# Attention written out over its 16 groups instead of a loop of three groups a pass

## The reference

```python
c_q = x @ W_dq
Q = (c_q @ W_uq).reshape(Bx, Sx, N_HEADS, D_K)
c_kv = x @ W_dkv
K = (c_kv @ W_uk).reshape(Bx, Sx, N_HEADS, D_K)
V = (c_kv @ W_uv).reshape(Bx, Sx, N_HEADS, D_K)
scores = jnp.einsum('bqhd,bkhd->bhqk', Q, K) / math.sqrt(D_K)
causal = jnp.tril(jnp.ones((Sx, Sx), dtype=bool))
scores = jnp.where(causal, scores, -jnp.inf)
attn = jax.nn.softmax(scores, axis=-1)
out = jnp.einsum('bhqk,bkhd->bqhd', attn, V).reshape(Bx, Sx, N_HEADS * D_K)
return out @ W_o
```

## Time and profile before

| | us |
|---|---|
| median of 3 runs | 1392.69 |
| lowest and highest run | 1389.38, 1393.0 |
| the profiled execution, its time | 1396.73 |
| the profiled execution, its span | 1395.0 |
| TensorE's first attention matmul of group 1, from the span's start | 527.38 |
| of group 3, the first in the loop | 588.83 |
| of group 12, the first behind the loop | 885.40 |
| of group 14, which has a list of its own | 947.64 |

### The profile page before, as it was taken

The page is one execution under the profiler, slowest core; times in us unless marked ns, Lnnn a source line. Parts: engine busy times, 40 slices in busy tenths (PEclk is TensorE's granted clock), DMA queues, the critical chain, the costliest instruction groups (busy, mean ns, idle before and its releaser), DMA issues. The chain is left out here.

```text
span 1395.0 us, 25999 instructions
## 1 busy us (share of the span) xinstructions
PE 1117.4 (80%) x7114; PEld 677.1 (49%) x7116; DVE 859.1 (62%) x2534; ACT 672.0 (48%) x1676; POOL 451.0 (32%) x456
## 2 busy tenths in 40 slices
PE   3548889884887599999899899999778289989860
PEld 2246777773333134444344344434256267778750
DVE  4773333333895688888788788888056743333327
ACT  3523434433456056766566566767636234444430
POOL 3635666663234400000000000000047456666640
PEclk9999999997778589999999999999989569999985
DMA  7602222224545903444434444340066012222229
GB/s 230 210 1 68 87 88 87 86 87 145 191 163 133 152 2 56 69 67 69 65 48 64 62 55 56 55 55 10 18 202 206 23 49 88 88 88 84 89 90 334
DMA packets 109455, 133.23 MB, mean 96 GB/s; under 512 B 30032, under 2 KB 83728, under 8 KB 109328
## 3 DMA queue, kind: packets, MB, share of 16 engines
q1 hardware_dynamic: 91280, 89.65, 28.6%
q0 software_dynamic: 13824, 37.77, 8.5%
q10 hardware_dynamic: 4224, 4.19, 0.9%
HBM read 82.68 MB, written 48.50 MB: 94 GB/s over the span
## 5 line engine op out<-in xcount | busy, mean ns | idle before, releaser
L1368 ACT ACTIVATE t_prob<-t_psS 128x512 f32<-128x512 f32 (+3 forms) x768 | 327.9, 494 | 191.0 <-PE t_psS L1300 160.1
L1388 DVE CUSTOM_DVE_ANT_0 t_psR<-t_psR,all_causal 128x128 f32<-128x128 f32 (+3 forms) x512 | 247.4, 503 | 63.6 <-PE t_psR L1278 58.9
L1278 PE MATMUL t_psR<-stacks_kst,stacks_qst 96*128 96x512 bf16 (+3 forms) x768 | 235.9, 347 | 32.7 <-PEq L851 16.1
L1297 PE MATMUL t_psS<-stacks_qst,stacks_kst 99*128 99x512 bf16 (+3 forms) x768 | 225.6, 334 | 2.2 <-ACT t_prob L1368 1.5
L1392 DVE TENSOR_REDUCE t_maxp<-t_psR 128x1 f32<-128x512 f32 x256 | 175.8, 687 | 20.9 <-PE t_psR L1278 20.6
L1278 PEld LDWEIGHTS t_psR<-stacks_kst,stacks_qst 96*128 96x128 bf16 x768 | 70.3, 98 | 214.3 <-DVE t_maxp L1388 108.0
L1311 PE MATMUL t_psO<-t_prob,t_vst 128*32 128x512 f32 (+3 forms) x1536 | 163.7, 498 | 3.0 <-ACT t_prob L1368 1.1
L1268 POOL COPY t_vst<-stacks_values 128x512 f32 (+1 forms) x16 | 9.8, 615 | 442.7 <-DMA stacks_kst<-qk_parts 442.4
L644 PE MATMUL ae_psG<-a_w,ae_xT 128*128 x432 | 116.4, 406 | 15.5 <-issue 9.8
L644 PE MATMUL be_psG<-b_w,be_xT 128*128 x432 | 117.4, 409 | 13.6 <-issue 9.1
L1300 PE MATMUL t_psS<-all_causal_t,all_ident_bf 128*128 128x128 bf16 x512 | 110.2, 222 | 0.0
(11 more groups left out here) (284 smaller groups left out, 1909.6 us busy)
## 6 DMA issues: line engine op xcount, KB each, us to landing
qk_parts<-q_parts SPq DMA_DIRECT2D x32, 384.0 KB, 2.6
stacks_qst<-qk_parts SPq DMA_DIRECT2D x96, 128.0 KB, 4.7
stacks_kst<-qk_parts SPq DMA_DIRECT2D x96, 128.0 KB, 7.1
q_yk<-y_rows SPq DMA_DIRECT2D x16, 512.0 KB, 6.0
s_yk<-y_rows SPq DMA_DIRECT2D x16, 512.0 KB, 9.3
o_rows<-t_orow SPq DMA_DIRECT2D x32, 136.0 KB, 7.6
bl_raw<-o_rows SPq DMA_DIRECT2D x8, 544.0 KB, 3.8
xn_rows<-al_xn SPq DMA_DIRECT2D x8, 512.0 KB, 3.9
```

The lines of the kernel that those rows point to most:

```text
L1278: nc.tensor.matmul(psR[bank][:, 0:w], qst[slot][0:KROWS, h, i * P:(i + 1) * P], kst[slot][0:KROWS, h, k0:k0 + w], start=True, stop=True).t ...
L1297: ins = nc.tensor.matmul(ps, kst[k][0:MROWS, h, j * P:(j + 1) * P], qst[k][0:MROWS, h, a:(c + 1) * 512], start=True, stop=a > j * P)
L1368: nc.scalar.activation(prob[j % 2][:, h, a:(c + 1) * 512], psS[n % ST_BANKS][:, a - c * 512:512], ACT.Exp, scale=DK ** -0.5).then_inc(exp_ ...
L1388: ins = nc.vector.tensor_tensor_reduce(psR[bank][:, 0:w], psR[bank][:, 0:w], T.causal[:, 512 - w:512], 1.0, -BIG, ALU.add, ALU.max, maxp[: ...
```

## The change

The loop is gone: every engine's code now goes over all 16 groups with the group number as a constant, so all waits compare with constants, no register is computed, and `hold` counts nothing. The planner's lists are made once and looked up. Tiles, banks, slots and the order of work stay as they were.

```diff
@@ phase_attention @@
+        plans = {(later, with_before): plan_step(units, later, with_before)
+                 for later, with_before in {(min(2, NG - 1 - g), g > 0) for g in range(NG)}}
...
             def run(eng):
-                last = (NG - 1) // SLOTS - 1
-                for k in range(SLOTS):
-                    step(k, k, 2, k > 0)
-                with eng.Fori(1, last) as it:
-                    for k in range(SLOTS):
-                        step(it * SLOTS + k, k, 2, True)
-                for g in range(last * SLOTS, NG):
-                    step(g, g % SLOTS, min(2, NG - 1 - g), True)
+                for g in range(NG):
+                    step(g, g % SLOTS, min(2, NG - 1 - g), g > 0)
             return run
...
         def ring_bank(g, idx):
-            return (idx + (ring_base(g) if isinstance(g, int) else RING0 - 2)) % RING_BANKS
+            return (idx + ring_base(g)) % RING_BANKS
...
-                for what, *at in plan_step(units, later, with_before)[0]:
+                for what, *at in plans[later, with_before][0]:
```

More of the change, by code:

```diff
@@ L1190, in run @@
             def run(eng):
-                last = (NG - 1) // SLOTS - 1
-                for k in range(SLOTS):
-                    step(k, k, 2, k > 0)
-                with eng.Fori(1, last) as it:
-                    for k in range(SLOTS):
-                        step(it * SLOTS + k, k, 2, True)
-                for g in range(last * SLOTS, NG):
-                    step(g, g % SLOTS, min(2, NG - 1 - g), True)
+                for g in range(NG):
+                    step(g, g % SLOTS, min(2, NG - 1 - g), g > 0)
             return run
         def ring_base(g):
-            if isinstance(g, int) and g == 0:
+            if g == 0:
                 return RING0
-            return g * RING + (RING0 - 2 - (AHEAD if isinstance(g, int) and g == NG - 1 else 0))
+            return g * RING + (RING0 - 2 - (AHEAD if g == NG - 1 else 0))
         def ring_bank(g, idx):
-            return (idx + (ring_base(g) if isinstance(g, int) else RING0 - 2)) % RING_BANKS
+            return (idx + ring_base(g)) % RING_BANKS
         def out_at(g, c):
-            if isinstance(g, int) and g == NG - 1:
+            if g == NG - 1:
                 return ring_base(g) + 2 + c + 1
-            later = min(2, NG - 2 - g) if isinstance(g, int) else 2
-            return ring_base(g + 1) + (plan_step(units, later, True)[1].index(("o", c)) + 1)
+            return ring_base(g + 1) + (plans[min(2, NG - 2 - g), True][1].index(("o", c)) + 1)
         @block.sync
@@ L1237, in step @@
                     load_max(g + 1, (k + 1) % SLOTS)
-                if not isinstance(g, int) or g + SLOTS < NG:
+                if g + SLOTS < NG:
                     hold(sp, pv_done, g * PV + PV, T)
@@ L1419, in step @@
                 base = ring_base(g)
-                for idx, (what, at, *ahead) in enumerate(plan_step(units, later, with_before)[1]):
+                for idx, (what, at, *ahead) in enumerate(plans[later, with_before][1]):
                     r, bank = base + idx, ring_bank(g, idx)
```

## The result

The changed kernel takes 1368.43 us (median of 4 runs, 1363.75 to 1371.37) against 1391.04 us of the kernel before in the same comparison (4 runs, 1384.49 to 1393.0). The ratio is 0.9839, with a 95% interval of 0.9811 to 0.9866: a gain of 22.6 us, by the interval 19 to 26. I had forecast 18.4 us, a time of 1374.3 and a range of 1369.5 to 1380.5.

A forecast was written before the change was run, and what follows sets the result against it. TensorE's matmuls bound written-out attention groups; the loop added steps and branch pauses. Of 20.0 us (7.7 register steps and holds, 11.9 way round, 0.4 late maxima), less 1.6 late maxima, 18.4 off 1392.69 gave 1374.3 us, range 1369.5 to 1380.5.

The forecast's parts named there:

- a shift of the phases behind attention by 3.6 us: Phases behind attention: one branch in their moved code gains or loses a pause, giving 1370.7 or 1377.9 us; chance 0.05.
- late maxima: Group starts in attention: 2 of 9 groups wait 0.78 us for DMAs of row maxima, 1.6 us off the gain.
- The price of the middle groups, by the written-out ones: Groups 3 to 11: each becomes a written-out group of 30.73 us, 20.0 us less than the 296.57 in the loop.
- Register arithmetic and counted holds: Loop groups 3 to 11: removing these steps on TensorE and VectorE saves 0.85 us a group, 7.7 us over nine.
- The bound of 2.6 us: VectorE in a loop group: removed register and semaphore instructions sum to 2.6 us, the most their removal could save.
- The way round: Groups 5, 6, 8, 9 around TensorE's two taken branches: 11.9 us go, 7.2 pauses and 4.7 lower clock.
- its cover: VectorE's loop branch, beside its wait for TensorE: counted at nothing; with that cover gone, 74 ns would be the price.
- Instruction loading: Attention written out as longer code: fetching it costed at nothing; should the cover be gone, 3.6 us and the clock behind.
- Late maxima in every group: Rival, SyncE's DMAs in attention: all nine groups start late, 7.0 us instead of 1.6, giving 1379.7 us; chance 0.15.
- hidden steps: Rival, loop groups: register steps were hidden all along, the 0.85 us a group stays, giving 1382.0 us; chance 0.05.
- a pause that is not the branch's: Rival, TensorE in attention: the pause recurs each third group whatever the branch and stays, giving 1386.2 us; chance 0.03.
- late blocks of code: Rival, TensorE's straight code: waits for blocks cost 6.0 us each, five give 1404.2 us, slower; chance 0.02.

## Why the prediction was right or wrong

**Where it failed: the other phases, put at nothing in the sum and at 3.6 us in the range.** The sum let every phase but attention stand still, and the range allowed the rest only this: the runs before lie 3.6 us apart, "which I allow on both sides of the forecast". The one rival of this kind, a shift of the phases behind attention by 3.6 us, looked the wrong way: behind attention 0.9 us came on, and ahead of it 7.7 us went, in code that the change doesn't touch. The time came out 5.9 us under the forecast of 1374.3. Of this 1.65 us is the base, whose median fell from 1392.69 to 1391.04 with a fourth run, and 4.2 us is a larger gain, 22.6 and not 18.4. About 1 of the 4.2 is the late maxima, below; the other 3 to 4 lie outside groups 3 to 11. Three runs had shown too little: with the fourth the kernel before spans 8.5 us (1384.49 to 1393.0), and the changed kernel 7.6.

On the other chips, where the phases ahead and behind lie within some 2 us of each other, the gain was 19.0 and 20.2 us by the medians (ratios 0.9856 and 0.9843). That the 3 to 4 us over the forecast are chance is argued, not shown, since the difference of 7.7 us was not reproduced and its cause stays open. What speaks for chance is the spread of this same code. The expert phase, from its first product into `psG` (line 644) to its last, takes 208.7 us ahead of attention and 207.5 behind it in the profile before, 205.2 and 206.5 in the one after. From the queries' first product to attention's it is 110.8 against 107.1 us there, and between 104.5 and 108.1 in the nine profiles on the other chips, where the kernels written out (106.4 to 108.1) are no faster than the one with the instructions of the kernel before (106.4).

**The price of the middle groups, by the written-out ones: right.** 20.0 us less late maxima was forecast, 19.3 measured over groups 3 to 11 in the first profile, and 20.1 in each of the two others (296.8 less 276.7 and 276.8).

**Register arithmetic and counted holds, 0.85 us a group: right in size, not told apart.** It is VectorE's (31.55 us with it alone looped, 30.73 with TensorE alone looped), and of VectorE's steps the counts: 0.71 of 0.83. The bound of 2.6 us that added up the instructions' durations said nothing about this; the place of an instruction, ahead of a wait or behind it, fits what was measured.

**The way round, 11.9 us: right.** The announced branch took the pauses and the lower clock away together. It gave 9.7 us in the time of the whole kernel and 11.2 us over groups 3 to 11 (296.8 - 285.7). The sentence that the branch costs nothing on VectorE but 74 ns if its cover is gone was wrong: it is 3.6 and 4.0 us. That this did no harm to the forecast is luck of the edit, which took the loop away from every engine at once.

**Late maxima, 1.6 us: too high.** In groups 3 to 11 they cost 0.7, 0.1 and 0.2 us in the three written-out profiles, and group 12 paid 1.3, 0.8 and nothing. One late group of four was too few to size it by; the choice made the forecast of the gain about 1 us too small.

**Instruction loading, nothing: right.** No idle piece without a releaser is left on TensorE in attention; the 17 fetches of straight code in groups 3 to 11 stay hidden.

**The rivals.** Late maxima in every group, hidden steps, a pause that is not the branch's, and late blocks of code are all refuted by the groups' rows above. The phases behind attention did not shift by a pause either (0.9 us). The Trainium skill's page "Advanced Engine Details and Errata", section "Control Flow Timing", has about 108 ns for a compare-and-branch; the runs gave 80 ns where it falls through, about 240 where it was announced, and 3600 to 4000 where not. The Trainium skill's page "Runtime: NRT & Kernel Launch", section "Instruction fetch mechanics", names the mechanism, a taken branch to a page that isn't there, and the runs bear it out: two transfers on q8 just behind the branch where the pause is, and none where the branch is announced.

## What to carry to other kernels

Price a loop's unrolling by groups that the same trace already runs in straight code: instructions, waits and contention are then all in the price, and the sum of the removed instructions' durations (5.7 us a group here) isn't needed and would mislead. Look at a long loop's closing branch by itself, in time and in the clock behind it, and announce it before writing the loop out: one instruction a pass and engine gave half of the gain here. When an engine alone keeps a loop, look for an idle piece behind its branch, not at the branch's own duration. Keep bookkeeping out from between a wait and the instruction that it holds, where its whole time came through here; and let a range be as wide as the phases that the change doesn't touch, which takes more than three runs to see.

## What was unexpected of the hardware

A short branch instruction does not mean a cheap branch. On VectorE the compare-and-branch lasts 62 ns, and the engine stands idle for 2.7 us behind it; in the row of the branch itself nothing of this is seen.

Thirty-two semaphore instructions of 21 ns lengthened a group by 0.71 us though VectorE is busy for only 27.2 of 30.7 us: with three banks going round, a delay behind a wait reaches TensorE, whose weight loads waited 1.5 us more for row maxima. And 98 instructions of 32 ns on TensorE's sequencer, 3.1 us a group on the engine that bounds the phase, lengthened it by nothing that the trace shows.

Announcing the branch not only hid the fetch on TensorE, it ended it: about 1700 instructions of loop body (1713 records on TensorE in groups 3 to 5) were read in the first pass and not again in two more, where the same loop unannounced took nine transfers in each. VectorE's announced loop lost its idle piece too, but the queue that rises when VectorE alone is looped, q14, still carried 19 transfers over groups 3 to 11, against 21 unannounced and 11 in straight code.
